# Two routed feed-forward layers: input rows fetched per expert tile through an inverted slot table, outputs written to token rows

## The reference, cut to what matters

```python
def _L0_ffn_ref(hidden_states, Wr, W1, b1, W2, b2):      # 8 experts, F = 1024, one expert per token
    router_probs = jax.nn.softmax(x @ Wr, axis=-1)
    expert_idx = jnp.argmax(router_probs, axis=-1)
    p_max = jnp.max(router_probs, axis=-1, keepdims=True)
    def expert_mlp(w1, bb1, w2, bb2):
        h = jax.nn.gelu(x @ w1 + bb1, approximate=False)
        return h @ w2 + bb2
    outs = jax.vmap(expert_mlp)(W1, b1, W2, b2)
    out = p_max * (the row of outs of expert_idx)
def _L1_ffn_ref(X, W1, b1, W3, b3, W2, b2, Wg, bg, Wf, bf):   # 8 experts, F = 512, two experts per token
    gating = jax.nn.softmax(X @ Wg + bg, axis=-1)
    top_k_indices = jnp.argsort(gating, axis=-1)[..., -TOPK:]
    h = jax.nn.silu((X @ W1 + b1) * (X @ W3 + b3))
    expert_outputs = h @ W2 + b2
    mixed = jnp.sum(topk_w[..., None] * topk_out, axis=2)
    return mixed @ Wf + bf
x = x + jnp.tanh(g_ffn[0]) * _L0_ffn_ref(_layernorm(x), ...)
x = x + jnp.tanh(g_ffn[1]) * _L1_ffn_ref(_layernorm(x), ...)
```

## Time and profile before

| | us |
|---|---|
| three executions | 3438.01, 3432.93, 3437.6 |
| median | 3437.6 |
| span of the profiled execution | 3429.7 |
| PE, DVE, ACT, POOL busy in it | 2900.1, 1886.9, 1407.8, 608.0 |
| L0 feed-forward | from about 96 to 331 |
| L1 feed-forward | from about 788 to 1167 |

### The profile page before, as it was taken

One profiled execution on the slowest core, in us unless ns is written; L12 is line 12 of the kernel. 1 busy time (PEld: TensorE's weight loads), 2 busy tenths in 40 slices (PEclk: granted clock), 3 DMA queues, 4 the chain that ended last, 5 costly groups with the idle time before them and its releaser, 6 DMA issues. The chain is left out here.

```text
span 3429.7 us, 46832 instructions
## 1 busy us (share of the span) xinstructions
PE 2900.1 (85%) x13932; PEld 2111.7 (62%) x13933; DVE 1886.9 (55%) x3558; ACT 1407.8 (41%) x2923; POOL 608.0 (18%) x571
## 2 busy tenths in 40 slices
PE   6495879972898798999789999999999998355997
PEld 5495545532786487999556666666666665233664
DVE  4312555403454336444478888888888886352332
ACT  1141544420221114444447777776777776100110
POOL 0202111113102120000201111111111111144554
PEclk7698889985998598999889999999999999577998
DMA  1443010005222101000010001000011000425775
GB/s 37 168 144 96 1 27 14 14 1 217 84 99 77 35 1 50 25 24 0 10 28 21 22 14 35 14 21 20 15 25 24 22 14 2 168 81 152 173 172 134
DMA packets 158692, 195.46 MB, mean 57 GB/s; under 512 B 39057, under 2 KB 129320, under 8 KB 154952
## 3 DMA queue, kind: packets, MB, share of 16 engines
q1 hardware_dynamic: 122072, 131.88, 12.8%
q0 software_dynamic: 22192, 40.13, 4.9%
q10 hardware_dynamic: 14304, 22.02, 1.9%
HBM read 105.38 MB, written 67.80 MB: 50 GB/s over the span
## 5 line engine op out<-in xcount | busy, mean ns | idle before, releaser
L1849 ACT ACTIVATE l3a_pt_hi<-l3a_banks 128x512 fp32r<-128x512 f32 (+2 forms) x640 | 382.0, 597 | 316.7 <-PE l3a_banks L1795 253.8
L1956 DVE TENSOR_TENSOR l3a_pt_lo<-l3a_pt,l3a_pt_hi 128x512 fp32r<-128x512 f32 (+2 forms) x640 | 460.3, 724 | 90.5 <-ACT l3a_pt L1850 85.9
L1850 ACT ACTIVATE l3a_pt<-l3a_banks 128x512 f32<-128x512 f32 (+2 forms) x640 | 378.0, 591 | 0.0
L1930 DVE TENSOR_REDUCE l3a_maxima<-l3a_banks 128x1 f32<-128x1178 f32 x256 | 351.4, 1376 | 2.4 <-PE l3a_banks L1746 1.1
L1795 PE MATMUL l3a_banks<-l3a_pt_hi,l3a_v 128*65 128x512 f32 (+2 forms) x640 | 286.3, 447 | 7.7 <-ACT l3a_out L1864 7.7
L1805 PE MATMUL l3a_banks<-l3a_q,l3a_k 128*128 128x512 f32 (+2 forms) x640 | 256.8, 401 | 7.2 <-ACT l3a_pt L1850 3.3
L1806 PE MATMUL l3a_banks<-l3a_q,l3a_k 72*128 72x512 f32 (+5 forms) x640 | 253.6, 396 | 0.0
L1795 PE MATMUL l3a_banks<-l3a_pt_hi,l3a_v_lo 128*65 128x512 f32 (+2 forms) x640 | 252.6, 395 | 0.0
L1795 PE MATMUL l3a_banks<-l3a_pt_lo,l3a_v 128*65 128x512 f32 (+2 forms) x640 | 252.4, 394 | 0.0
L1746 PE MATMUL l3a_banks<-l3a_k,l3a_q 128*128 128x512 f32 (+1 forms) x768 | 216.2, 392 | 15.4 <-DVE l3a_maxima L1930 14.3
L1746 PEld LDWEIGHTS l3a_banks<-l3a_k,l3a_q 128*128 128x128 f32 x768 | 141.8, 195 | 61.6 <-DVE l3a_maxima L1930 39.3
(11 more groups left out here) (524 smaller groups left out, 6053.1 us busy)
## 6 DMA issues: line engine op xcount, KB each, us to landing
l3f_w<-in_L_ffn_w SPq DMA_DIRECT2D x96, 256.0 KB, 3.2
l0f_w<-in_L_ffn_W ACTq DMA_DIRECT2D x12, 1024.0 KB, 6.6
l3f_slots_x<-l3f_empty SPq DMA_DIRECT2D x10, 1168.0 KB, 14.3
l3f_x_rows<-l3f_slots_x SPq DMA_DIRECT2D x32, 292.0 KB, 3.9
l1f_w<-in_L_ffn_W ACTq DMA_DIRECT2D x18, 512.0 KB, 4.6
l2f_w<-in_L_ffn_w SPq DMA_DIRECT2D x16, 512.0 KB, 4.7
l3a_q<-l3a_q SPq DMA_DIRECT2D x64, 128.0 KB, 2.3
l3a_k<-l3a_k SPq DMA_DIRECT2D x64, 128.0 KB, 2.3
```

The lines of the kernel that those rows point to most:

```text
L1849: act.activation(a.pt_hi[0:rows, n % a.pt_slots, :], a.st_bank[0:rows, n % 2, :], ACT.Exp, bias=bias, scale=scale)
L1850: act.activation(a.pt[0:rows, n % 4, :], a.st_bank[0:rows, n % 2, :], ACT.Exp, bias=bias, scale=scale).then_inc(a.exped, 1)
L1930: dve.tensor_reduce(a.maxima[:, n:n + 1], banks.rearrange("p a b -> p (a b)")[:, 0:KEYS], AX.X, ALU.max).then_inc(a.maxed, 1)
L1956: dve.tensor_tensor(a.pt_lo[0:rows, slot, :], a.pt[0:rows, n % 4, :], a.pt_hi[0:rows, slot, :].bitcast(F32), ALU.subtract).then_inc(a.lo_m ...
```

## The change

Nothing is scattered into slots any more. DVE and PE turn the map "slot of each token" round into "token of each slot": a token's slot is cut into a lane (its low 7 bits) and a column (the rest). For each tile of tokens DVE builds a one-hot matrix of lanes and a matrix that holds the token's number (minus 2048) in its column, and PE sums their products over all tiles, which gives a table of 128 lanes x 26 columns (L0) or 42 columns (L1). An empty slot is zero and becomes one of 128 spare rows that hold zeros. In L1 the sign of an entry tells the first from the second choice. The normalized rows are stored in token order in DRAM, and POOL fetches each expert tile's 128 rows by an indirect DMA, one tile ahead; its indices are a column that DVE copies out of the table. POOL scatters each y_tile straight to token rows (`sums` in L0; `outs` in L1, one region of 2048 rows per choice), and the end reads them with plain DMAs. In L1 the bias bf is added to x before the loop, scaled by the gate, and PE turns the mixed tile t + 1 before it multiplies tile t.

```diff
+def show_slots(dve, step, sem, place, slot, lane, column, lanes, columns, ids, at_column, of_token, at_lane):
+    step(dve.tensor_copy(slot, place))
+    step(dve.tensor_scalar(lane, slot, P - 1, None, ALU.bitwise_and))
+    step(dve.tensor_scalar(column, slot, 7, None, ALU.logical_shift_right))
+    step(dve.tensor_tensor(at_column, spread(column, width), columns.unsqueeze(1).to_broadcast([P, entries, width]), ALU.is_equal))
+    step(dve.tensor_tensor(of_token, at_column, spread(ids, width), ALU.mult))
+    for n in range(0, entries, TABLE_CHUNK):
+        dve.tensor_tensor(at_lane[:, n:n + TABLE_CHUNK, :], spread(lane[:, n:n + TABLE_CHUNK], P),
+                          lanes.unsqueeze(1).to_broadcast([P, TABLE_CHUNK, P]), ALU.is_equal).then_inc(sem, 1)
+def invert_slots(pe, out, at_lane, values, ready=None):
+    for n in range(entries):
+        if ready is not None and n % TABLE_CHUNK == 0:
+            pe.wait_ge(ready, n // TABLE_CHUNK + 1)
+        ins = pe.matmul(out, at_lane[:, n, :], values[:, n, :], start=n == 0, stop=n == entries - 1)
+def token_table(dve, step, sums, own, spare, table):
+    step(dve.scalar_tensor_tensor(spare, sums, 0.0, own.to_broadcast([P, sums.shape[1]]), ALU.is_equal, ALU.mult))
+    step(dve.scalar_tensor_tensor(table, sums, float(TOKENS), spare, ALU.add, ALU.add))
...
 def l1_ffn(nc, chip, I):
...
         def _(sp):
...
-            for slots in (slots_x, slots_y):
-                for t in range(0, SLOT_TILES, 8):
-                    n = min(8, SLOT_TILES - t)
-                    sp.dma_start(slots[t * P:(t + n) * P, :].rearrange("(p n) d -> p (n d)", p=P), zeros[:, 0:n * D]).then_inc(cleared, 16)
-            for u in range(2):
-                load_expert(sp, u, u)
-            sp.wait_ge(placed, 1)
-            sp.wait_ge(scattered, 16 * K * TILES)
-            sp.dma_start(x_tile[:], slots_x[0:P, :]).then_inc(x_loaded, 16)
...
-                    sp.wait_ge(x_turned, at)
-                    sp.dma_start(x_tile[:], slots_x[bass.ds(at * P, P), :]).then_inc(x_loaded, 16)
+            sp.dma_start(rows[TOKENS:TOKENS + P, :], zeros[:]).then_inc(rows_kept, 16)
+            load_expert(sp, 0, 0)
+            for q in range(4):
+                sp.wait_ge(turn.staged, 4 * (q + 1))
+                sp.dma_start(rows[4 * q * P:4 * (q + 1) * P, :].rearrange("(t p) d -> p t d", p=P), chip.xn[:, 4 * q:4 * (q + 1), :]
+                             ).then_inc(rows_kept, 16)
+            load_expert(sp, 1, 1)
+            sp.wait_ge(all_stored, 1)
+            for q in range(4):
+                load_outputs(sp, 0, q)
...
         def _(pool):
...
-            for t in range(TILES):
-                for k in range(K):
-                    pool.indirect_dma_start(slots_x, bass.IndirectOffsetOnAxis(index[k][:, t:t + 1], 0), chip.xn[:, t, :], None
-                                            ).then_inc(scattered, 16)
+            pool.wait_ge(rows_kept, 80)
             pool.wait_ge(placed, 1)
+            pool.indirect_dma_start(x_tile[:], None, rows, bass.IndirectOffsetOnAxis(in_table[:, 0:1], 0)).then_inc(x_loaded, 16)
+            pool.wait_ge(indexed, 1)
+            pool.indirect_dma_start(x_tile[:], None, rows, bass.IndirectOffsetOnAxis(in_index[:], 0)).then_inc(x_loaded, 16)
             g = one_register(pool, "l1f_pool_g")
             with pool.Fori(0, E) as e:
                 with tiles_of_expert(pool, tile_counts, e, g, MAX_TILES) as at:
+                    pool.wait_ge(indexed, at + 1)
+                    pool.sem_inc(taken, 1)
+                    pool.indirect_dma_start(x_tile[:], None, rows, bass.IndirectOffsetOnAxis(in_index[:], 0)).then_inc(x_loaded, 16)
                     pool.wait_ge(y_kept, at + 1)
-                    pool.dma_start(slots_y[bass.ds(at * P - P, P), :], y_tile[:]).then_inc(y_stored, 16)
+                    pool.sem_inc(taken, 1)
+                    pool.indirect_dma_start(outs, bass.IndirectOffsetOnAxis(out_index[:], 0), y_tile[:], None).then_inc(y_stored, 16)
                     pool.wait_ge(y_stored, at * 16)
                     pool.sem_inc(y_free, 1)
...
         def _(pe):
...
-                pe.matmul(p_h[:, 2 + t % 2, 0:D], chip.ones[0:1, :], bf[:], start=False, stop=True).then_inc(out_done, 1)
+            turn_mixed(0)
+            for t in range(TILES):
+                if t + 1 < TILES:
+                    turn_mixed(t + 1)
+                pe.wait_ge(mixed_kept, t + 1)
...
         def _(act):
...
+            act.wait_ge(all_stored, 1)
+            for q in range(4):
+                load_outputs(act, 1, q)
...
         def _(dve):
...
             def keep_turned(turnings):
                 dve.wait_ge(x_turned, turnings)
                 dve.tensor_copy(xt_tile[:], p_xt[:, 0:D]).then_inc(x_kept, 1)
+                dve.tensor_copy(in_index[:], column(in_table, turnings)).then_inc(indexed, 1)

             keep_turned(1)
+            for t in range(0, TILES, 4):
+                dve.tensor_tensor(chip.x[:, t:t + 4, :], chip.x[:, t:t + 4, :], gbf[:].unsqueeze(1).to_broadcast([P, 4, D]), ALU.add
+                                  ).then_inc(biased, 1)
...
                     dve.wait_ge(y_done, at + 1)
                     dve.wait_ge(y_free, at)
+                    dve.tensor_copy(out_index[:], column(out_table, at - 1))
                     dve.tensor_tensor(y_tile[:], p_y[:, 0:D], tile_of(b2, e), ALU.add).then_inc(y_kept, 1)
```

More of the change, by code:

```diff
@@ L681, in _ @@
             dve.wait_ge(exped, 1)
+            dve.wait_ge(constants, 7)
+            choose(dve, step, exps[:], chosen[:], order[:], place[:], best[:], 0)
+            dve.sem_inc(chose, 1)
             step(dve.tensor_reduce(weight[:], exps[:], AX.X, ALU.add))
@@ L700, in keep_turned @@
                 dve.tensor_copy(xt_tile[:], p_xt[:, 0:D]).then_inc(x_kept, 1)
+                dve.tensor_copy(in_index[:], column(table, turnings)).then_inc(indexed, 1)
             keep_turned(1)
```

258 lines of the change are left out of this document (152 added, 106 removed).

## The result

The changed kernel took 3369.8 us (median of four executions, 3365.3 to 3375.2), the kernel before 3435.3 in the same group of runs (3432.2 to 3438.0). The ratio is 0.981 (95% interval 0.980 to 0.983): 65 us faster, where 92 were forecast. The time lies in the range given, 24 us above the forecast. The span of the profiled execution went from 3429.7 to 3373.5; the profiled execution of the changed kernel is the slowest of its four, so the spans lie 56 us apart and the medians 65.

A forecast was written before the change was run, and what follows sets the result against it. Bounds: POOL's scatters ahead of each layer's first turn, PE in the loops and at half clock in L1's tail. 15.9 + 12.2 + 31.7 + 39.8 - 8 = 91.6 saved; forecast 3346 us, range 3330 to 3374.

The forecast's parts named there:

- the heads: Table building and one gather replace scatters ahead of each layer's first turn: 15.9 us saved in L0, 31.7 in L1.
- the tails: Ends of both layers after the last y_tile: 12.2 us saved in L0, 39.8 in L1.
- the 8 products behind the last wide step: End of table building in the heads: PE's remaining products, with the way there and back, taken as 1.5 us.
- the chain, the gather behind a late store on POOL: Loops, at weight loads: the next gather queues behind a store landing after up to 6.5 us; 12.5 against 11.24.
- I take 1 us for each of the 6 loads in L1 and 1 in all for L0: Loss at weight loads in the expert loops (bounds 0 and 3 each), part of 8 us lost in all.
- The gather in flight may be slowed as well: Loops, at weight loads: a row gather already under way may also land later; no size of its own.
- DVE's pace, 28 in my working: L1's tail at full clock: DVE's steps set 1.45 us a tile, 28 in all; half clock 41; 33 taken.
- work without a gap: L1's tail: PE, always having work, might reach full clock as behind L1's first turn; 33 us taken.
- A plain tile costs nothing: Loops: gather and scatter chains fit, 1.2 us to spare in L1; DVE's index copies lie in idle time.
- The port rule: L1's first turn: POOL's second gather waits for DVE's four bias additions; second tile some 2 us late.
- POOL sets the pace in L1's loop: Rival: indirect DMAs taking 4.2 us to land need 6.0 a tile against 5.62; 3361 to 3370, chance 0.18.
- the three signs that I had named against myself: Wrong if: PE waits for x_tile in ordinary tiles; loop indirect DMA over 4 us; tail 4 us a tile.

The follow-up runs named there:

- Experiment 1: Changed kernel with POOL's wait for the previous tile's y scatter moved behind the next row gather in both layers: 3338.6 us, ratio 0.971 to the kernel before.
- the second pair: The changed kernel and the one with POOL's wait behind the next row gather, run again in one group: 3365.2 and 3333.5 us.
- experiments 6 and 7: On the changed kernel, L1's tail: 6 adds bf by a product again, 3398.2 us; 7 puts each turn right ahead of its own product again, 3372.4 us.

## Why the prediction was right, and where it was wrong

The path of each stretch was in the main as predicted, and the sizes were off. Over the stretches the heads gave 8.8 us less than forecast, the loops cost 26.0 more, and the tails gave 5.7 more; that the time still fell into the range is in part luck, since the tails paid some of it back and since the range went up to 3374 for a rival that was not the case.

*Heads: the mechanism held, the size was short by 4.4 us each.* The path was as described. L0's PE started 11.5 earlier and not 15.9, L1's 27.3 and not 31.7. Of the two misses of 4.4 the rows give these parts. The products of the table made DVE wait 2.55 and 3.70 where 1.5 was taken (bounds 1.2 and 2.7). The term that was mis-sized: I counted only the 8 products behind the last wide step, but PE at 1.2 GHz does not keep up with DVE, so that in L1 all 32 of them, 7.0 us, set the end. The router's products, which the change leaves as they are, took 10.97 in L0 against 8.65 (granted clock 0.63 against 0.82) and 11.28 in L1 against 9.73, with a turning stretch ahead of them 0.5 and 0.9 longer. And POOL began 0.97 and 0.88 after the last table step, while I carried over the 0.36 that a scatter took the earlier trace rows.

*Loops: the largest error, 26 us.* I had named the chain, the gather behind a late store on POOL, and then sized it badly. "I take 1 us for each of the 6 loads in L1 and 1 in all for L0" is the step that failed. Worked out with the rows above for L0: y_tile is ready at T + 4.5 and not at L1's T + 2.8, which I used for both layers when I wrote that L0 fits better; 0.8 to the issue of the scatter; 6.9 to landing; 2.2 from there to the issue of the gather, for which I had put 0.3 (between 200.50, when y_free reached DVE, and 202.49 the code takes POOL through the end of a loop and the read of a new tile count; no row times these by themselves); 2.8 for the gather. Together 17.2, which is 205.25 less 188.01, against 14.5 for two tiles: 2.7 late, of which 1.9 show as PE's wait at this load. In L1 the same chain at the load of 969.08 is 2.9 + 0.8 + 5.7 + 2.0 + 2.9 = 14.3 (966.71 to 980.98), where I had 12.5. So the two hand-overs on POOL, put at 0.15 and 0.3 and measured at 0.8 and 2.0 to 2.2, are what the sum lacked in both layers, and in L0 the later y_tile besides. The sum of the waits is 11.6 in L0 and 13.5 in L1, of which 2.4 in L1 are the two slow gathers, the one case that my sentence "The gather in flight may be slowed as well" had left open. Behind some of the waits the clock falls. Of the rest of the loss, 1.3 us in L0 and 0.9 in L1 are the first tile. Experiment 1 changed nothing in the loops but POOL's order, and their loss, from first to last turn, went from 33.8 to 2.5 (in the second pair from 27.4 to 3.8).

*The tails.* L0's came out at 12.3 (12.2 forecast). L1's gave 45.4 instead of 39.8, since the clock rose after 7 us: DVE's pace, 28 in my working, was the case, it took 25.6, and I had taken a value between; mixing began 1.8 later than worked out. The reason I gave for it, work without a gap, did not hold (experiments 6 and 7).

*A plain tile costs nothing:* right; ordinary tiles of L1 take 5.6 to 5.7 us, and gathers and scatters away from a load land in 2.4 to 2.8.

*The port rule.* While the four additions to x ran on DVE, POOL's issue of the second gather took 1.68 us instead of 0.99 in L0, but it began 0.36 us after the start of the additions (835.13 and 835.49), not behind them, and the second tile did not wait for it. The Trainium skill (SBUF — State Buffer, § SBUF: two separate sides) has such a step hold the ports, against an instruction of POOL that reads SBUF, until it ends. The rows agree with a delay by the rest of one step: 0.7 us longer, where the first step had 0.8 left. That rule is about one instruction; that all four would stand ahead of POOL I had added myself, and the 2 us later second turn did not come.

*The rivals.* None of those given was the case as a whole. The measured total lies where "POOL sets the pace in L1's loop" had it, 3361 to 3370, by another mechanism: no ordinary tile was late, and the places are the loads and the first tile. Of the three signs that I had named against myself one appeared, an indirect DMA in the loop that needs over 4 us (6.9); PE's waits in ordinary tiles and a tail of 4 us a tile did not.
